# A four-block hybrid network on one core: where the mixture blocks make and store their base, how they end, and how the mixer starts

## The reference

```python
x = x + mixer(_layernorm(x))       # selective scan: 256 channels, 16 states
x = x + mixture(_layernorm(x))     # 8 experts
x = x + attention(_layernorm(x))   # linear: Q (K^T V), no softmax
x = x + mixture(_layernorm(x))     # same weights
...
def mixture(x):                              # x is normalised already
    scores = (tanh(x @ gate_w.T) + 1) * 0.5
    vals, idx = top_k(scores.T, 512)         # each expert takes 512 tokens
    y = _layernorm(x[idx], ln_gamma, ln_beta)
    h = gelu(y @ fc1.T + b1)
    o = (h @ fc2.T + b2) * vals
    return x.at[idx].add(o)
```

## Time and profile before

| | us |
|---|---|
| device time, median of 3 runs (915.99 to 918.4) | 916.13 |
| profiled execution | 916.01 |
| its span | 914.0 |
| PE busy | 660.9 (72%) |
| DVE busy | 602.2 (66%) |
| POOL busy | 574.0 (63%) |
| ACT busy | 487.0 (53%) |
| mixer | 0 to 506 |
| first mixture | 506 to 688 |
| attention | 689 to 732 |
| second mixture | 733 to 914 |

### The profile page before, as it was taken

How to read it: one execution, slowest core, us unless ns; L and a number is a source line. 1 busy time by engine, 2 the same in 40 slices (tenths; PEclk the granted TensorE clock), 3 DMA queues, 4 the chain that set the end, 5 groups by cost and what they waited for, 6 DMA issues and landing times. The chain is left out here.

```text
span 914.0 us, 11670 instructions
## 1 busy us (share of the span) xinstructions
PE 660.9 (72%) x3803; PEld 495.0 (54%) x3803; DVE 602.2 (66%) x1101; ACT 487.0 (53%) x941; POOL 574.0 (63%) x443
## 2 busy tenths in 40 slices
PE   3898987899878998789886564799422952289941
PEld 1366666676567765667675343566312841266631
DVE  6587778887798876979995888532104498843210
ACT  1588796787867878787980464123103247013310
POOL 6059768697596976879985420788750051078874
PEclk9979997899988999879978775599775876569976
DMA  5135445444433544543651633133323005123332
GB/s 140 69 106 174 136 134 174 139 158 143 141 139 139 161 140 139 163 161 118 204 188 47 209 92 98 45 45 41 39 23 99 1 1 161 30 53 41 43 33 22
DMA packets 68698, 95.60 MB, mean 105 GB/s; under 512 B 15289, under 2 KB 48866, under 8 KB 68642
## 3 DMA queue, kind: packets, MB, share of 16 engines
q1 hardware_dynamic: 56818, 85.19, 28.9%
q0 software_dynamic: 11264, 8.66, 7.2%
q10 hardware_dynamic: 560, 1.05, 0.4%
HBM read 81.73 MB, written 13.11 MB: 104 GB/s over the span
## 5 line engine op out<-in xcount | busy, mean ns | idle before, releaser
L356 POOL TENSOR_TENSOR product<-state,c_all 128x1024 f32<-128x1024 f32 x128 | 301.4, 2375 | 115.1 <-DVE state L594 98.4
L594 DVE TENSOR_TENSOR_SCAN state<-decay,m_psum 128x1024 f32<-128x1024 f32 x64 | 145.1, 2281 | 33.7 <-PE m_psum L768 20.9
L594 DVE TENSOR_TENSOR_SCAN state<-decay,carry,m_psum 128x1024 f32<-128x1024 f32 x64 | 147.8, 2337 | 21.5 <-issue 9.9
L435 ACT ACTIVATE drive_T<-dtu_T,b_T 128x128 f32<-128x128 f32 x448 | 142.1, 390 | 37.2 <-PE m_psum L768 36.8
L742 PE MATMUL m_psum<-ident,product 128*128 128x128 f32 x1024 | 146.4, 290 | 5.8 <-POOL product L356 5.7
L477 ACT ACTIVATE decay<-dt,decay_rate 128x1024 f32<-128x1024 f32 x128 | 144.6, 1138 | 2.9 <-DVE state L594 2.8
L1098 ACT ACTIVATE f_f_T<-f_psum,shared_b_T 128x512 f32<-128x512 f32 x64 | 44.0, 687 | 175.3 <-PE f_psum L1408 175.1
L742 PEld LDWEIGHTS m_psum<-ident,product 128*128 128x128 f32 x1024 | 123.4, 150 | 24.9 <-issue 14.9
L840 POOL DMA_INDIRECT f_got<-f_table,f_tokens x64 | 66.0, 1032 | 100.0 <-DVE f_tokens L1249 41.9
L768 PE MATMUL m_psum<-ident,drive_T 128*128 128x128 f32 x640 | 93.3, 294 | 23.4 <-DVE state L594 15.0
L768 PEld LDWEIGHTS m_psum<-ident,drive_T 128*128 128x128 f32 x640 | 80.1, 152 | 45.7 <-DVE state L594 23.9
(11 more groups left out here) (198 smaller groups left out, 993.3 us busy)
## 6 DMA issues: line engine op xcount, KB each, us to landing
c_all<-c_dram SPq DMA_DIRECT2D x128, 512.0 KB, 3.9
f_table<-f_rows SPq DMA_DIRECT2D x2, 2176.0 KB, 9.6
X<-in_L_attn_a_x SPq DMA_DIRECT2D x4, 512.0 KB, 7.4
f_w_raw<-in_L_ffn_fc2s SPq DMA_DIRECT2D x1, 2048.0 KB, 16.7
between<-f_f SPq DMA_DIRECT2D x1, 2048.0 KB, 8.7
X<-between SPq DMA_DIRECT2D x4, 512.0 KB, 7.5
out<-f_f SPq DMA_DIRECT2D x1, 2048.0 KB, 8.7
carry<-state SPq DMA_DIRECT2D x64, 0.5 KB, 1.7
```

The lines of the kernel that those rows point to most:

```text
L356: pool.tensor_tensor(product[:, n % RING, :], state[:, n % RING, :], c_all[:, n % RING, :], ALU.mult).then_inc(product_ready, 1)
L435: act.activation(drive_T[:, turn % TURNS, i], dtu_T[:, k, i], ACT.Copy, scale=b_T[:, g % 2, i, s:s + 1]).then_inc(act_drive, 1)
L594: dve.tensor_tensor_scan(state[:, n % RING, :], decay[:, n % RING, :], pair(n).rearrange("p a t -> p (a t)"), 0.0 if starts_batch(g) else ...
```

## The change

- **Mixer's front.** ACT normalises the first chunk's 8 tiles instead of DVE; DVE goes on to the statistics of the second chunk and copies the first two turned banks. PE starts with 20 matmuls of the identity with itself. PE's wait for the last weights moves from ahead of u to the piece "mixed". PE broadcasts B of states 0 and 1 before the pieces b_T and dtu_T, and ACT makes the decays of these states before it copies them (EAGER = 2).
- **Base.** POOL's four adds go. ACT writes X + f as one Identity activation for each tile, with the scale rstd + 1, which one small DVE operation makes (scale_1). These 32 activations follow the rows and, in f1, the weight copies. There three rows go to one copy, and the last six copies follow the rows.
- **Stores.** The table is stored first, the base second. The gathers wait for the table alone; the first scatter and DVE's first writes into o wait for the base's store.
- **End.** SP waits for the scatters instead of POOL. The block is made without POOL's Drain at its end; the Drains around the clearing of the semaphores stay. In f1, SP issues the four loads of X for attention before the block's barrier; attention waits for them by semaphores that outlive f1. The statistics start by quarter.

```diff
+            def fade(n):
+                g, k, s = place(n)
+                act.activation(decay[:, n % RING, :], dt[:, k, :], ACT.Exp,
+                               scale=decay_rate[:, k, s:s + 1]).then_inc(decay_ready, 1)
+
             std(0, 1)
-            take_turned(0)
-            take_turned(1)
+            act.wait_ge(ln_ready, 1)
+            for i in range(CT):
+                act.activation(xn[:, i, :], X[:, i, :], ACT.Identity, bias=shift[:, i:i + 1],
+                               scale=rstd[:, i:i + 1]).then_inc(normed, 1)
             std(1, CHUNKS)
...
+                if piece[0] == "bT":
+                    act.wait_ge(rate_ready, 1)
+                    act.wait_ge(turned, BATCH * L // BANK)
+                    act.wait_ge(dt_ready, 1)
+                    for n in range(EAGER):
+                        fade(n)
                 take(piece, number)
...
+            at = scale_and_shift(0, 1, token_stats(0, at))
+            at = token_stats(1, at)
+            for g in range(TB):
+                take_turned(g)
+            for g in range(2, CHUNKS):
                 at = token_stats(g, at)
-            at = normalise(1, CHUNKS, at)
+            at = scale_and_shift(1, CHUNKS, at)
+            dve.wait_ge(ln_ready, 2)
+            for i in range(CT, CHUNKS * CT):
+                dve.tensor_scalar(xn[:, i, :], X[:, i, :], rstd[:, i:i + 1], shift[:, i:i + 1],
+                                  ALU.mult, ALU.add).then_inc(normed, 1)
...
+            WARM = 20
+            for i in range(WARM):
+                pe.matmul(psum[:, PIECE, 0:P], ident[:], ident[:], start=True, stop=True)
+            def broadcast(n):
+                g, k, s = place(n)
+                for t in range(TB):
+                    last = pe.matmul(pair(n)[:, t, :], pick_r[SPLIT:P, s, :],
+                                     b_split[SPLIT:P, g % 2, t * BANK:(t + 1) * BANK],
+                                     start=True, stop=True)
+                last.then_inc(b_bcast, 1)
+
+            assert all(maker(n) == "dve" for n in range(EAGER))
...
                 if kind == "bT":
                     for g in range(TB + 1, BATCH * L // BANK):
                         turn(g)
+                    pe.wait_ge(xnT_ready, BATCH * L // BANK)
+                    pe.wait_ge(b_ready, TB)
+                    for n in range(EAGER):
+                        broadcast(n)
                 if kind == "u":
                     pe.wait_ge(xnT_ready, t + 2)
                 if kind == "mixed":
+                    pe.wait_ge(w_loaded, 16 * 7)
                     pe.wait_ge(w_all_ready, 1)
...
+                    if n < EAGER:
+                        pass
+                    elif maker(n) == "dve":
+                        broadcast(n)
...
-            block = ctx.enter_context(nc.Block())
+            block = ctx.enter_context(nc.Block(no_gpsimd_drain=True))
...
-                sp.wait_ge(base_ready, 4)
-                sp.dma_start(dst.rearrange("(i p) d -> p i d", p=P), f[:]).then_inc(stored, 16)
                 sp.wait_ge(rows_ready, TILES)
                 sp.wait_ge(weights_ready, HALVES)
-                sp.dma_start(table.rearrange("(i p) d -> p i d", p=P), rows[:]).then_inc(stored, 16)
-                sp.wait_ge(stored, 32)
+                sp.dma_start(table.rearrange("(i p) d -> p i d", p=P), rows[:]).then_inc(table_stored, 16)
+                sp.wait_ge(base_ready, TILES)
+                sp.dma_start(dst.rearrange("(i p) d -> p i d", p=P), f[:]).then_inc(base_stored, 16)
+                sp.wait_ge(table_stored, 16)
+                sp.wait_ge(base_stored, 16)
                 if first_use:
                     sp.wait_ge(loaded, 16 * 5)
+                for r in range(2):
+                    sp.wait_ge(scattered[r], 16 * KT * TWO)
+                quarter = TILES // 4
+                for n, landed in enumerate(reloaded):
+                    sp.dma_start(X[:, n * quarter:(n + 1) * quarter, :],
+                                 dst[n * quarter * P:(n + 1) * quarter * P, :].rearrange("(i p) d -> p i d", p=P)
+                                 ).then_inc(landed, 16)
...
-                quarter = TILES // 4
-                for n in range(4):
-                    part = slice(n * quarter, (n + 1) * quarter)
-                    pool.wait_ge(f_turned, (n + 1) * quarter // 4)
-                    pool.tensor_tensor(f[:, part, :], X[:, part, :], f[:, part, :],
-                                       ALU.add).then_inc(base_ready, 1)
-
-                pool.wait_ge(stored, 32)
-                pool.sem_inc(o_free, AHEAD)
+                pool.wait_ge(table_stored, 16)
...
                     pool.wait_ge(o_ready, e + 1)
-                    if e:
-
+                    if e == 0:
+                        pool.wait_ge(base_stored, 16)
+                    else:
                         pool.wait_ge(scattered[(e - 1) % 2], 16 * KT * ((e - 1) // 2 + 1))
                         pool.sem_inc(o_free, 1)
...
-                pool.wait_ge(scattered[(E - 1) % 2], 16 * KT * TWO)
-                pool.wait_ge(scattered[(E - 2) % 2], 16 * KT * TWO)
...
+                ROWS = 3
                 for i in range(TILES):
                     act.activation(rows[:, i, 0:DM], X[:, i, :], ACT.Identity, bias=shift2[:, i:i + 1],
                                    scale=rstd2[:, i:i + 1]).then_inc(rows_ready, 1)
-                    if first_use and i % 2:
-
-                        n = i // 2
-                        e, layer = divmod(n, 2)
-                        act.wait_ge(w_turned, n + 1)
-                        where = w2_T[:, e].rearrange("p q d -> p (q d)") if layer else w1_T[:, e, :]
-                        act.copy(where, psum[:, W_TURN + n % 2, :]).then_inc(w_taken, 1)
+                    if first_use and i % ROWS == ROWS - 1:
+                        take_w(i // ROWS)
+                if first_use:
+                    for n in range(TILES // ROWS, 2 * E):
+                        take_w(n)
+                act.wait_ge(f_turned, NB)
+                act.wait_ge(scale1_ready, 1)
+                for i in range(TILES):
+                    act.activation(f[:, i, :], X[:, i, :], ACT.Identity, bias=shift[:, i:i + 1],
+                                   scale=scale_1[:, i:i + 1]).then_inc(base_ready, 1)
...
+                dve.tensor_scalar(scale_1[:], rstd[:], 1.0, None, ALU.add).then_inc(scale1_ready, 1)
...
-                    dve.wait_ge(o_free, e + 1)
+                    if e < AHEAD:
+                        dve.wait_ge(base_stored, 16)
+                    else:
+                        dve.wait_ge(o_free, e + 1 - AHEAD)
...
+                if first_use:
+                    pe.wait_ge(w_taken, 2 * E)
...
-            for n in range(4):
-                sp.dma_start(X[:, n * QT:(n + 1) * QT, :],
-                             source[n * QT * P:(n + 1) * QT * P, :].rearrange("(i p) d -> p i d", p=P)
-                             ).then_inc(x_loaded[n], 16)
             for out, what in ((q_w[:], wq), (kv_w[:, 0, :], wk), (kv_w[:, 1, :], wv), (o_w[:], wo)):
                 sp.dma_start(out, what).then_inc(loaded, 16)
...
+                    for i in range(n * QT, (n + 1) * QT):
+                        dve.bn_stats(stats[:, i, :], X[:, i, :]).then_inc(chain, 1)
+                at += TB
+                dve.wait_ge(chain, at)
```

More of the change, by code:

```diff
@@ L174, in mamba @@
         EARLY = 3
+        EAGER = 2
         def maker(n):
@@ L1456, in attention @@
         mix = sb("mix", [P, BATCH, DM])
-        x_loaded = [sem(f"x_loaded{n}") for n in range(4)]
         loaded = sem("loaded")
@@ L1648, in build @@
                                       ("w1_T", [P, E, FF]), ("w2_T", [P, E, FF // P, DM]))}
-        moe(nc, X, ident, shared, "f1", between, True, **experts)
-        attention(nc, X, ident, between, **linear)
-        moe(nc, X, ident, shared, "f2", out.rearrange("b l d -> (b l) d"), False, **experts)
+        reloaded = [ctx.enter_context(nc.semaphore(f"reloaded{n}")) for n in range(4)]
+        moe(nc, X, ident, shared, "f1", between, True, reloaded, **experts)
+        attention(nc, X, ident, reloaded, **linear)
+        moe(nc, X, ident, shared, "f2", out.rearrange("b l d -> (b l) d"), False, (), **experts)
 _INS = ["L0_attn_a_x", "L0_attn_a_W_in", "L0_attn_a_conv_w", "L0_attn_a_conv_b", "L0_attn_a_A_log",
```

53 lines of the change are left out of this document (25 added, 28 removed).

## The result

The changed kernel takes 896.25 us (median, 895.97 to 896.45) against 916.06; the ratio is 0.978, interval 0.976 to 0.980: 19.8 us faster, where 9.0 were forecast. The time is within the range, and next to that of rival G (896.5), which had 0.19.

The account below looks back on a forecast made before the run. Four engines share the mixer's bound; no engine computes in the 14.3 us gap after the first mixture, other openings are waits. Gains 2.8 + 2.9 + 1.3 + 2.0 = 9.0 took 916.0 to 907.0 us, range 895.0 to 911.0.

Parts of the forecast that it names:

- rival G: Mixtures' ends: the 5.28 us belong to the removed POOL Drain, no later one pays; 896.5 us in all, chance 0.19.
- The Drain: Mixtures' ends: a later POOL Drain pays the 5.3 us; −2.0 from first mixture to attention, 0 at the second end.
- M: The forecast itself: the Drain's price is paid later by another Drain; 907.0 us, own range 904.5 to 911, chance 0.47.
- Mixer: Mixer's front: earlier u, B broadcasts and decays ahead save 2.8 us, range 1.2 to 5.3.
- s: Mixer's front: gain at the start of PE's u matmuls, between 0.45 and 2.5 us, taken as 1.0.
- the held case: Mixer's front: POOL's cast holds DVE's small operation behind the statistics; u starts at 16.4 instead of 17.3, 0.9 earlier.
- the middle between ACT's and DVE's lead: Mixer behind u: gain taken as 1.8 us, between ACT's 0.75 and DVE's 2.8.
- N: Rival: the mixer absorbs its front's gain, 909.8 us; with gathers behind the store 913.1; chance of 911 to 915: 0.12.
- Store on the gathers: First mixture: the base's store overlaps the first expert's gathers; loss taken as 0, up to 3.3 us if they land behind it.
- Table first: First mixture only: the table is stored before the base, so the first gather starts earlier; −1.3 us.
- Fronts: Fronts of both mixtures: without POOL's four adds DVE is not held; −1.45 us each, −2.9 together.
- S: Rival, slower: TensorE's lower clock level falls elsewhere in the mixer's long part; 922.0 us, chance 0.04.

## Why the prediction was wrong

- **The Drain, −2.0 and 0 forecast.** The step that failed is the reading that "the later one pays it". No later Drain took over 0.13 us; taking it out gave 5.25 and 5.23. Rival G, which I put at 0.19 because "a Drain of the same kind stays", was the mechanism: Drains that look alike in the rows don't cost alike, and the one at the block's end is the costly one. I had weighed equal rows as a sign for M; they fit G as well.
- **Mixer, −2.8 forecast with 1.2 as the least.** s was right for u's start in the first trace (0.8 for 1.0, the held case), in part by luck: in the second u started at 15.04 and its matmuls ended no earlier. The first scan came even 3.5 earlier. The step that failed is the middle between ACT's and DVE's lead: I priced the two decays on ACT at 0.4 for "the copies that now come later" and did not follow who waits for these copies. PE's dt for the second half and, behind it, the third state do. Nine traces end the mixer at 506.5 on average, those of before at 506.2, 507.0 and, without Drain, 506.4: nothing is left that a trace shows. That is what N said, and the reason is near N's: PE's matmuls of dt, behind which its long work follows, started no earlier (50.65 on average against 50.41).
- **Store on the gathers, 0 taken out of 0 to 3.3.** Measured 2.5. The bound was right, the choice was not: that four gathers are little beside the store does not keep them from waiting, and the store held the fourth for 3.6 us (5.15 against 1.58). The Trainium skill, "DMA: Bandwidth & Descriptors", Queues, rings and completion order, has a DMA engine take its queues in turn, packet by packet. The tenths that I worked out from that are not what the trace shows; the measurement decides.
- **Table first, −1.3.** 1.2 to the first gather. The gathers start 0.9 behind the tokens, not 0.3: these 0.6 are about the 0.5 that I had given back.
- **Fronts, −2.9.** 3.1 by the traces, 3.3 by the run with POOL's adds back: right, and for the reason given.
- **Gap beyond the Drain.** 3.4 more, where M had 2.0 for the whole gap and G 1.9 beside the Drain (7.2 less 5.3): 2.0 for loads or quarters, as in G, and 1.4, in no rival, for a shorter issue that came with the changed mixer and stays unexplained.
- **Attention.** 3.0, a draw of TensorE's clock in the trace that I started from, not in the sum at all. S named that danger with the other sign.

That the total fell on G's 896.5 is in part chance: the mixer (+1.9) and the store (+2.5) fell short by about what the gap's rest and attention's draw gave.

## What to carry to other kernels

Price every synchronising instruction at a block's end by taking it out alone, and again by putting it back into the finished kernel: a Drain behind gathers and scatters, 5.3 us each time, was worth 10.5 in the one and 3.1 in the other, where other waits cover it. Follow a step that is moved ahead to those that now stand behind it, up to the third user, before its lead is counted; and where a price runs from 0 to a store's full length, do not take 0 because the gathers beside it are small: here 2.5 of at most 3.3 came true. Look at two traces of the same kernel before explaining a stage that no edit touches.

## What the runs showed that I had not expected

- POOL's Drain at the block's end costs 5.3 us behind its gathers and scatters, from when POOL is through, and 0.1 behind the mixer's tensor operations; its record may open 6 us before (11.3 us long).
- TensorE's level drops for some 7 us in attention (0.66 over 10 us, so 6.8 of them at 0.50) in some traces and not in others, with the same work ahead: 3.0 us.
- The granted clock reads 1.00 from the start in the trace of before, although the first u matmuls take up to 1193 ns; in the changed kernel, whose u matmuls are as slow (up to 1193), the same stretch reads 0.50. The windows from 16 to 18 us, before and changed:

```profile
16.00:18.00 2.00, 1.23 (x3) 0.69 (x3) 1.97 (x14) 0.58 (x1) 0.75 (x2) 1.00 0.00 0
```

```profile
16.00:18.00 2.00, 1.51 (x2) 0.84 (x3) 1.97 (x10) 0.00 (x0) 0.84 (x2) 0.50 0.01 4
```

So a clock of 1.00 at the head of a trace is not to be read as measured there; the matmuls' own durations are.
